# Gated cross-attention and mixture-of-experts block on one core: how the first context chunk, the positions and the later context chunks are loaded and split

## The chip, the core and the metric

The kernel runs on one core of a Trainium2 chip. The metric is device time in microseconds (us). TensorE (PE) multiplies matrices, VectorE (DVE), ScalarE (ACT) and GpSimd (POOL) do elementwise work, SyncE (SP) issues most DMAs. Each engine has its own queue of instructions and they meet at semaphores.

## The reference, cut to what matters

```python
x   = x + tanh(g_xattn) * xattn(layernorm(x), ctx, ctx, positions, mask, Wq, Wk, Wv, Wo)
x   = x + tanh(g_ffn)   * ffn(layernorm(x), gate_w, gate_b, w1, b1, w2, b2)

# xattn: x and ctx are [8, 128, 512]; 32 query heads, 8 key/value heads of 128; all fp32
q = (query @ Wq)                    # Wq [512, 4096]
k = (ctx @ Wk); v = (ctx @ Wv)      # Wk, Wv [512, 1024]
cos, sin = cos_t[position_ids], sin_t[position_ids]   # tables of 512 positions
q, k = q * cos + rotate_half(q) * sin, k * cos + rotate_half(k) * sin
attn = softmax(where(mask == 0, -1e9, q @ k.T / sqrt(128)))
xattn = (attn @ v) @ Wo             # Wo [4096, 512]
# ffn: three experts (tanh, gelu, silu) of 512x512 matrices, two of them chosen for each sample
```

The positions matter below only through the gather of their rows of the cos/sin table (rope).

## The kernel before

Every fp32 matrix is split into a high half (a copy rounded to fp32r by ACT or DVE) and a low half (the value minus the high half, by DVE or POOL). A product is then three matmuls: high by high, low by high, high by low. Names with `_hi` and `_lo` belong to these, and so do the semaphores: `c_hi` and `c_lo` count context chunks, `w_hi` and `w_lo` weight chunks.

The context comes as eight chunks (`ctx_in`), each 128 channels by 4 samples by 128 tokens: chunks one to four are the four parts of the contraction for samples 0 to 3, five to eight those for samples 4 to 7. SP loads them into four buffers `rows` (256 KB each), ACT and DVE split them into `cT` (a part of `big`). Weights come in chunks of 128 by 512 into four buffers `wraw` and are split into `wa` and `wb` (parts of `big` too). ACT issues the load of Wv's first chunk itself, and SP all other loads.

PE starts with `BLANKS` dummy matmuls on a zeroed tile (L562), then `first_values` forms the values of samples 0 to 3 in four banks (`y0`, `y1` and the two halves of `s`), chunk by chunk, so that each chunk is used when it comes:

```python
for c in range(EC - 1):
    pe.wait_ge(c_hi, c + 1)
    pe.wait_ge(w_hi, c + 1)
    if c == 0:
        pe.wait_ge(w0_half, 1)
    for b in range(BH):
        part(c, b, 0, 0)
    pe.wait_ge(c_lo, c + 1)
```

Then come 23 tiles of keys and values in an order written out by hand (`TILE_ORDER`): one value tile, then the first key tile, which has `rope_transpose(0)` and `(1)` ahead of it and `(2)` and `(3)` behind it. These are transposes of the gathered table rows, which POOL brings with eight indirect DMAs (L1161), four into `rot` and four into `prob`; the gathers wait for `pos_ok`, which DVE raises after four small operations on the positions (L1320 to L1327). All the rest of the program, 64 units of attention and then the experts, follows on PE in a fixed order.

Of the kernel before, what the change touches and what calls it, by code (L numbers as in the profile page):

```python
# [37 lines left out]
P = 128  # L38
B = 8
E = 512  # L40
EC = E // P
# [24 lines left out]
FILL = LAG_S  # L66
BLANKS = 9
LN_AT = (7, 11, 13, 14)
# [21 lines left out]
def build(nc, x, ctx_in, pos, mask, g_xattn, g_ffn, Wq, Wk, Wv, Wo, gate_w, gate_b, w1, b1, w2, b2,  # L90
          rope_rows, k_scratch, v_scratch, out):
    with ExitStack() as stack:
# [6 lines left out]
        def sem(name):  # L99
            return stack.enter_context(nc.semaphore(name))  # L100
# [57 lines left out]

        c_in = [sem(f"c_in{k}") for k in range(NROW)]
        c_hi, c_lo = sem("c_hi"), sem("c_lo")  # L160
        x_in = [sem(f"x_in{b}") for b in range(B)]
        small_in = sem("small_in")
        pos_in = sem("pos_in")
        mask_in = sem("mask_in")
        w_in = [sem(f"w_in{k}") for k in range(NW)]
        w_hi, w_lo, w0_half = sem("w_hi"), sem("w_lo"), sem("w0_half")
        pool_const, ident_ok, blank_ok = sem("pool_const"), sem("ident_ok"), sem("blank_ok")
# [100 lines left out]
        def piece(s, k):  # L268

            half, c = k // EC, k % EC  # L270
            return cT[s][half][:, :, c, :]

        def staged(k):
            return rows[:, k % NROW, :].rearrange("p (b t) -> p b t", b=BH)

# [125 lines left out]
        def _(sp):  # L401
# [5 lines left out]
            def c_load(k):  # L407
                if k >= NROW:
                    sp.wait_ge(c_lo, k - NROW + 1)
                sp.dma_start(rows[:, k % NROW, :], ctx_in[k // EC, k % EC]).then_inc(c_in[k % NROW], 16)  # L410

            for k in range(EC):
                c_load(k)
                if k >= 1:
                    w_load(k, w_chunks[k]).then_inc(w_in[k % NW], 16)
                else:
                    sp.dma_start(posi[:, :], pos).then_inc(pos_in, 16)
            for n in range(EC, W_DVE):
# [4 lines left out]
            for m in range(-AHEAD, TILES_A):  # L423
# [4 lines left out]
                if m < 0:  # L428
                    continue
                if m < B:  # L430
                    sp.dma_start(xacc[:, m, :], x[m]).then_inc(x_in[m], 16)
                if m == B:
# [73 lines left out]
        def _(pe):  # L506
# [21 lines left out]
            def first_values():  # L528
# [5 lines left out]
                for c in range(EC - 1):  # L534
                    pe.wait_ge(c_hi, c + 1)
                    pe.wait_ge(w_hi, c + 1)
                    if c == 0:
                        pe.wait_ge(w0_half, 1)
                    for b in range(BH):
                        part(c, b, 0, 0)  # L540
                    pe.wait_ge(c_lo, c + 1)
                    for b in range(BH):
                        part(c, b, 1, 0)
                    pe.wait_ge(w_lo, c + 1)
                    for b in range(BH):
                        part(c, b, 0, 1)
# [290 lines left out]
        def _(act):  # L837
# [27 lines left out]
            def c_hi_(k):  # L865
                act.wait_ge(c_in[k % NROW], 16 * (k // NROW + 1))
                act.activation(piece(0, k), staged(k), ACT.Copy).then_inc(c_hi, 1)
# [22 lines left out]

            act.dma_start(wraw[:, 0, :], w_chunks[0]).then_inc(w_in[0], 16)
            c_hi_(0)
            act.wait_ge(w_in[0], 16)
            act.activation(w_target(0)[0][0][:, 0, 0:256], wraw[:, 0, 0:256], ACT.Copy).then_inc(w0_half, 1)
            act.wait_ge(w_hi, 1)
# [381 lines left out]
        def _(dve):  # L1277
# [31 lines left out]
            def w_lo_(n):  # L1309
# [4 lines left out]
            dve.wait_ge(w_in[0], 16)  # L1314
            dve.tensor_copy(w_target(0)[0][0][:, 0, 256:512], wraw[:, 0, 256:512]).then_inc(w_hi, 1)
            c_lo_(0)
            dve.wait_ge(w0_half, 1)
            w_lo_(0)
            dve.wait_ge(pos_in, 16)
# [8 lines left out]
                              ).then_inc(pos_ok, 1)  # L1328

            for k in range(1, EC):  # L1330
                c_lo_(k)
                w_lo_(k)
# [480 lines left out]
```

## Time and profile before

| | |
|---|---|
| median of 3 runs | 701.52 us (701.26 to 702.04) |
| the profiled execution, its own time | 702.05 us |
| its span, first to last instruction | 700.3 us |
| PE busy | 691.8 us, 99% |
| DVE, ACT, POOL busy | 559.9, 361.4, 402.7 us |
| mean granted clock of PE | 0.997 |

The profile is of one execution, and its own time stands beside the runs. A row of the timeline gives an instruction's start, its duration, its engine and line, and in brackets how long the engine stood idle before it and who released it. A matmul of 512 columns is shown with a duration longer than its share of the pipeline, so that the spacing of starts says how fast PE goes.

### The profile page before, as it was taken

What the parts mean: (1) busy time and instruction counts of PE and PEld (TensorE: products, weight loads), DVE (VectorE), ACT (ScalarE), POOL (GpSimd) and SP (SyncE); (2) the same over time, 40 slices, a digit from 0 to 9 for tenths busy, and PEclk for the clock granted to TensorE, in tenths of its full rate; (3) what the DMA queues carried; (4) which work ended last, traced back from release to release, by engine and by line L of the source; (5) the groups of instructions that cost most, each with busy time, mean ns of one, the idle gap of its engine ahead of it and who ended that gap; (6) DMA issues with size and microseconds to landing.
All of it is one profiled execution on the core that took longest, in us unless ns stands there. A gap on an engine that the chain in (4) does not pass through costs nothing.

```text
span 700.3 us, 11567 instructions
## 1 busy us (share of the span) xinstructions
PE 691.8 (99%) x3479; PEld 580.2 (83%) x3479; DVE 559.9 (80%) x951; ACT 361.4 (52%) x961; POOL 402.7 (57%) x345
## 2 busy tenths in 40 slices
PE   9999999999999999999999999999999999999998
PEld 7888887888888888888888888888888887688886
DVE  5788786887887887887887887887887997687785
ACT  5525624545545545545555555555555687653521
POOL 5788855666666666666666566666566655330000
PEclk9999999999999999999999999999999999999999
DMA  8997564321231221221221221222222422120001
GB/s 264 345 307 287 196 205 141 107 89 61 63 91 61 62 90 60 64 86 60 66 84 62 67 83 60 68 82 60 72 80 61 136 90 76 60 77 31 1 31 60
DMA packets 65071, 70.84 MB, mean 101 GB/s; under 512 B 7680, under 2 KB 41472, under 8 KB 65024
## 3 DMA queue, kind: packets, MB, share of 16 engines
q1 hardware_dynamic: 64496, 68.98, 30.6%
q0 software_dynamic: 384, 1.05, 0.5%
q8 instruction: 19, 0.31, 0.2%
q10 hardware_dynamic: 144, 0.26, 0.1%
q14 instruction: 28, 0.23, 0.1%
HBM read 51.40 MB, written 18.87 MB: 100 GB/s over the span
## 4 chain that ended last, share of the span: by engine, by line
PE 89%; DVE 4%; ACT 2%; POOL 1%; issue 1%; SPq 1%; DMA 1%; DVEq 0%; ACTq 0%; POOLq 0%
PE q L298 29%; PE y L288 28%; PE q L288 6%; PE o L665 6%; PE s L647 5%; PE pt L509 4%; PE s L649 2%; PE o L288 2%; PE pt L288 2%; PE s L288 1%; PE s L509 1%; PE y L531 1%; PE s L531 1%; ACT prob L980 1%; DVE split L1279 1%
## 5 line engine op out<-in xcount | busy, mean ns | idle before, releaser
L288 PE MATMUL y<-big,split 128*128 128x512 f32 (+1 forms) x864 | 209.4, 391 | 0.7 <-DVE split L1279 0.5
L288 PEld LDWEIGHTS y<-big,split 128*128 128x128 f32 x864 | 161.0, 188 | 34.6 <-DVE split L1279 1.6
L298 PE MATMUL q<-xT_hi,big 128*128 128x512 f32 x512 | 175.1, 403 | 0.0
L1217 POOL TENSOR_TENSOR roped<-rot 128x512 f32<-128x512 f32 x58 | 75.1, 1294 | 101.7 <-DVE rot L1305 101.7
L966 ACT ACTIVATE big<-roped 128x512 fp32r<-128x512 f32 x63 | 40.0, 635 | 141.6 <-POOL roped L1217 136.4
L298 PEld LDWEIGHTS q<-xT_hi,big 128*128 128x128 f32 x512 | 96.1, 188 | 19.2
L980 ACT ACTIVATE prob<-scores,nmax 128x128 f32<-128x128 f32 x256 | 99.8, 391 | 20.4 <-DVE nmax L1437 20.3
L1231 POOL TENSOR_TENSOR prob<-prob,prec 128x512 f32<-128x512 f32 x64 | 66.7, 1042 | 60.5 <-DVE prec L1442 60.5
L298 PE MATMUL q<-xT_lo,big 128*128 128x512 f32 x256 | 99.5, 389 | 0.0
L1220 POOL TENSOR_TENSOR big<-roped,big 128x512 fp32r<-128x512 f32 x63 | 81.7, 1297 | 13.2 <-ACT big L966 13.2
L1209 POOL TENSOR_TENSOR big<-wraw,big 128x512 fp32r<-128x512 f32 x64 | 83.1, 1298 | 0.0
L1442 DVE RECIPROCAL prec<-psums 128x4 f32<-128x4 f32 x64 | 11.4, 178 | 66.1 <-ACT prob L980 65.8
L647 PE MATMUL s<-kv,big 128*128 128x256 f32 x256 | 62.6, 322 | 0.2 <-POOL big L1220 0.2
L949 ACT ACTIVATE split<-o 128x512 fp32r<-128x512 f32 x57 | 34.0, 597 | 54.3 <-PE o L665 54.3
L1301 DVE TENSOR_TENSOR rot<-q,rope 128x512 f32<-128x512 f32 x72 | 49.1, 682 | 10.6 <-PE q L298 8.8
L649 PE MATMUL s<-kv,big 128*128 128x128 f32 x256 | 57.0, 223 | 0.0
L1167 POOL TENSOR_TENSOR big<-wraw,big 128x512 fp32r<-128x512 f32 x32 | 41.1, 1296 | 27.0 <-ACT big L841 27.0
L298 PEld LDWEIGHTS q<-xT_lo,big 128*128 128x128 f32 x256 | 48.4, 189 | 8.7
L665 PE MATMUL o<-split,kv 128*128 128x512 f32 x192 | 54.4, 391 | 0.6 <-DVE split L1279 0.6
L1446 DVE SCALAR_TENSOR_TENSOR xacc<-y,gates,xacc 128x512 f32<-128x512 f32 x64 | 47.9, 748 | 5.2 <-PE y L288 1.2
L647 PEld LDWEIGHTS s<-kv,big 128*128 128x128 f32 x256 | 48.2, 188 | 3.3 <-POOL big L1220 0.8
L649 PEld LDWEIGHTS s<-kv,big 128*128 128x128 f32 x256 | 48.8, 191 | 2.4
(200 smaller groups left out, 1279.5 us busy)
## 6 DMA issues: line engine op xcount, KB each, us to landing
wraw<-in_L_xattn_Wq SPq DMA_DIRECT2D x32, 256.0 KB, 2.9
wraw<-in_L_xattn_Wo SPq DMA_DIRECT2D x32, 256.0 KB, 2.8
kv<-k_scratch SPq DMA_DIRECT2D x64, 128.0 KB, 2.5
kv<-v_scratch SPq DMA_DIRECT2D x64, 128.0 KB, 2.7
v_scratch<-split SPq DMA_DIRECT2D x12, 512.0 KB, 3.9
wraw<-in_L_ffn_w SPq DMA_DIRECT2D x24, 256.0 KB, 2.8
k_scratch<-split SPq DMA_DIRECT2D x10, 512.0 KB, 3.4
k_scratch<-kv SPq DMA_DIRECT2D x6, 512.0 KB, 3.5
```

Source lines behind the costliest of these rows:

```text
L288: mm = pe.matmul(bank_[:, :], stationary(s, c), moving(m, c), start=(c == 0 and n == 0), stop=(c == EC - 1 and n == 2))
L298: mm = pe.matmul(bank_[:, :].rearrange("p (b t) -> p b t", b=BH), weights[s][:, c, h * P:(h + 1) * P], source[m][:, half * BH:(half + 1) * ...
L647: pe.matmul(sbanks[:, 2 * h * P:(2 * h + 2) * P], q[0], kv[:, bs % NKV, 0:2, :].rearrange("p m k -> p (m k)"), start=True, stop=False)
L649: mm = pe.matmul(sbanks[:, 2 * h * P:(2 * h + 1) * P], q[1], kv[:, bs % NKV, 0, :], start=False, stop=True)
L665: mm = pe.matmul(obank[:, :], kv[:, bs % NKV, 2 + s, :], split[:, 1, m, :], start=(n == 0), stop=(n == 2))
L980: a = act.activation(prob[:, 0, h * P:(h + 1) * P], scores[:, h * P:(h + 1) * P], ACT.Exp, bias=nmax[:, turn, h:h + 1], accum_out=psums[:, ...
L1209: pool.tensor_tensor(buf[1][:, b % EC, :], wraw[:, b % NW, :], buf[0][:, b % EC, :].bitcast(F32), ALU.subtract).then_inc(w_lo, 1)
L1217: pool.tensor_tensor(roped[:, :], rot[:, 0, :], rot[:, 1, :], ALU.add).then_inc(q_roped, 1)
L1220: pool.tensor_tensor(q_split(1, bq // BH, bq % HG), roped[:, :], q_split(0, bq // BH, bq % HG).bitcast(F32), ALU.subtract).then_inc(q_lo, 1)
L1231: pool.tensor_tensor(heads(prob[:, 1, :]), heads(prob[:, 0, :]), prec[:, turn, :].unsqueeze(2).to_broadcast([P, HG, P]), ALU.mult).then_in ...
L1301: dve.tensor_tensor(to[:, 0, :], bank_[:, :], table(0, 0, D), ALU.mult)
L1446: dve.scalar_tensor_tensor(out=xacc[:, b3, :], in0=ybank[b3 % 2][:, :], scalar=gates[:, 0:1], in1=xacc[:, b3, :], op0=ALU.mult, op1=ALU.ad ...
```

## The change

It does six things.

- The first context chunk comes in two DMAs of 256 columns (samples 0 and 1, samples 2 and 3), with semaphores of their own (`c0_in`, `c_in[0]`), and ACT copies the halves one by one (`c0_half`, then `c_hi`).
- DVE makes the whole high half of Wv's first chunk (before, ACT and DVE made 256 columns each) and its low half at once behind it.
- PE takes the first chunk's products in another order: samples 0 and 1 high by high, then high by low, then the same of samples 2 and 3, then all four low by high.
- DVE handles the positions behind chunk two (index 1) instead of ahead of it; SP issues their load behind both halves of chunk one.
- Context chunks five to eight go into `xacc` (four of the buffers that later take x), so SP does not wait for a free buffer in `rows`; the loads of x into these four wait for `c_lo` instead.
- There are 7 dummy matmuls instead of 9.

```diff
-BLANKS = 9
+BLANKS = 7
...
         def staged(k):
-            return rows[:, k % NROW, :].rearrange("p (b t) -> p b t", b=BH)
+            return (rows[:, k, :] if k < NROW else xacc[:, k - NROW, :]).rearrange("p (b t) -> p b t", b=BH)
...
             def c_load(k):
-                if k >= NROW:
-                    sp.wait_ge(c_lo, k - NROW + 1)
-                sp.dma_start(rows[:, k % NROW, :], ctx_in[k // EC, k % EC]).then_inc(c_in[k % NROW], 16)
-
-            for k in range(EC):
+                sp.dma_start(staged(k), ctx_in[k // EC, k % EC].rearrange("p (b t) -> p b t", b=BH)
+                             ).then_inc(c_in[k], 16)
+
+            sp.dma_start(rows[:, 0, 0:2 * P], ctx_in[0, 0][:, 0:2 * P]).then_inc(c0_in, 16)
+            sp.dma_start(rows[:, 0, 2 * P:4 * P], ctx_in[0, 0][:, 2 * P:4 * P]).then_inc(c_in[0], 16)
+            sp.dma_start(posi[:, :], pos).then_inc(pos_in, 16)
+            for k in range(1, EC):
                 c_load(k)
-                if k >= 1:
-                    w_load(k, w_chunks[k]).then_inc(w_in[k % NW], 16)
-                else:
-                    sp.dma_start(posi[:, :], pos).then_inc(pos_in, 16)
+                w_load(k, w_chunks[k]).then_inc(w_in[k % NW], 16)
...
                 if m < B:
+                    if m < PIECES - NROW:
+                        sp.wait_ge(c_lo, NROW + m + 1)
                     sp.dma_start(xacc[:, m, :], x[m]).then_inc(x_in[m], 16)
...
                 for c in range(EC - 1):
-                    pe.wait_ge(c_hi, c + 1)
                     pe.wait_ge(w_hi, c + 1)
                     if c == 0:
-                        pe.wait_ge(w0_half, 1)
+
+                        pe.wait_ge(c0_half, 1)
+                        part(c, 0, 0, 0)
+                        part(c, 1, 0, 0)
+                        pe.wait_ge(w_lo, c + 1)
+                        part(c, 0, 0, 1)
+                        part(c, 1, 0, 1)
+                        pe.wait_ge(c_hi, c + 1)
+                        part(c, 2, 0, 0)
+                        part(c, 3, 0, 0)
+                        part(c, 2, 0, 1)
+                        part(c, 3, 0, 1)
+                        pe.wait_ge(c_lo, c + 1)
+                        for b in range(BH):
+                            part(c, b, 1, 0)
+                        continue
+                    pe.wait_ge(c_hi, c + 1)
...
             act.dma_start(wraw[:, 0, :], w_chunks[0]).then_inc(w_in[0], 16)
-            c_hi_(0)
-            act.wait_ge(w_in[0], 16)
-            act.activation(w_target(0)[0][0][:, 0, 0:256], wraw[:, 0, 0:256], ACT.Copy).then_inc(w0_half, 1)
+            act.wait_ge(c0_in, 16)
+            act.activation(piece(0, 0)[:, 0:2, :], staged(0)[:, 0:2, :], ACT.Copy).then_inc(c0_half, 1)
+            act.wait_ge(c_in[0], 16)
+            act.activation(piece(0, 0)[:, 2:4, :], staged(0)[:, 2:4, :], ACT.Copy).then_inc(c_hi, 1)
             act.wait_ge(w_hi, 1)
...
             dve.wait_ge(w_in[0], 16)
-            dve.tensor_copy(w_target(0)[0][0][:, 0, 256:512], wraw[:, 0, 256:512]).then_inc(w_hi, 1)
+            dve.tensor_copy(w_target(0)[0][0][:, 0, :], wraw[:, 0, :]).then_inc(w_hi, 1)
+            w_lo_(0)
+            dve.wait_ge(c0_half, 1)
             c_lo_(0)
-            dve.wait_ge(w0_half, 1)
-            w_lo_(0)
+            c_lo_(1)
+            w_lo_(1)
             dve.wait_ge(pos_in, 16)
...
-            for k in range(1, EC):
+            for k in range(2, EC):
                 c_lo_(k)
                 w_lo_(k)
```

On DVE, at the start of the program; `wraw` is a weight chunk as loaded, `rows` a context chunk, `posf` and `posi` the positions. Before:

```order
L1315 CAST big<-wraw 128x256 [waits w_in0]
L1279 TENSOR_TENSOR big<-rows,big 128x4x128 [waits c_hi]
L1279 TENSOR_TENSOR big<-wraw,big 128x512 [waits w_hi,w0_half]
L1320 CAST posf<-posi 128x8 [waits pos_in]
L1322 TENSOR_SCALAR posf<-posf 128x8 [waits pos_step]
L1325 TENSOR_TENSOR posf<-posf 128x8 [waits pos_step]
L1327 TENSOR_SCALAR posi<-posf 128x8 [waits pos_step]
L1279 TENSOR_TENSOR big<-rows,big 128x4x128 [waits c_hi]
L1279 TENSOR_TENSOR big<-wraw,big 128x512 [waits w_hi]
```

The same place after the change:

```order
L1333 CAST big<-wraw 128x512 [waits w_in0]
L1297 TENSOR_TENSOR big<-wraw,big 128x512 [waits w_hi]
L1297 TENSOR_TENSOR big<-rows,big 128x4x128 [waits c_hi,c0_half]
L1297 TENSOR_TENSOR big<-rows,big 128x4x128 [waits c_hi]
L1297 TENSOR_TENSOR big<-wraw,big 128x512 [waits w_hi]
L1340 CAST posf<-posi 128x8 [waits pos_in]
L1342 TENSOR_SCALAR posf<-posf 128x8 [waits pos_step]
L1345 TENSOR_TENSOR posf<-posf 128x8 [waits pos_step]
L1347 TENSOR_SCALAR posi<-posf 128x8 [waits pos_step]
```

Wv's low half has moved ahead of the context's, and the four operations on the positions stand behind two more subtractions.

On PE, from the dummies to the end of the first chunk. Before:

```order
L562 MATMUL o<-xT_hi 128x512 [waits blank_ok]
L562 MATMUL o<-xT_hi 128x512 x8
L531 MATMUL y0<-big 128x512 [waits w0_half,w_hi,c_hi]
L531 MATMUL y1<-big 128x512
L531 MATMUL s<-big 128x512 x2
L531 MATMUL y0<-big 128x512 [waits c_lo]
```

And after:

```order
L579 MATMUL o<-xT_hi 128x512 [waits blank_ok]
L579 MATMUL o<-xT_hi 128x512 x6
L533 MATMUL y0<-big 128x512 [waits c0_half,w_hi]
L533 MATMUL y1<-big 128x512
L533 MATMUL y0<-big 128x512 [waits w_lo]
L533 MATMUL y1<-big 128x512
L533 MATMUL s<-big 128x512 [waits c_hi]
L533 MATMUL s<-big 128x512 x3
L533 MATMUL y0<-big 128x512 [waits c_lo]
```

The banks `y0` and `y1` (samples 0 and 1) now get two products each before `s` (samples 2 and 3) gets its first. Behind the chunk nothing moves on PE.

On SP, the first issues of the program. Before:

```order
L410 DMA rows<-ctx_t 128x512
L417 DMA posi<-in_pos_BxS2 128x8
L410 DMA rows<-ctx_t 128x512
L405 DMA wraw<-in_L0_xattn_Wv 128x512
...
L410 DMA rows<-ctx_t 128x512 [waits c_lo] x4
L405 DMA wraw<-in_L0_xattn_Wk 128x512 [waits w_lo] x7
L431 DMA xacc<-in_x 128x512
```

And after:

```order
L412 DMA rows<-ctx_t 128x256
L413 DMA rows<-ctx_t 128x256
L414 DMA posi<-in_pos_BxS2 128x8
L409 DMA rows<-ctx_t 128x512
L406 DMA wraw<-in_L0_xattn_Wv 128x512
...
L409 DMA xacc<-ctx_t 128x512 x4
L406 DMA wraw<-in_L0_xattn_Wk 128x512 [waits w_lo] x7
L433 DMA xacc<-in_x 128x512 [waits c_lo]
```

One issue has come in ahead of chunk two, and the four context loads have lost their wait.

## Rows read from the trace of the kernel before

**Rows 1.** Totals of the page: busy time, share of the span, instructions.

```profile
PE 691.8 (99%) x3479; PEld 580.2 (83%) x3479; DVE 559.9 (80%) x951; ACT 361.4 (52%) x961; POOL 402.7 (57%) x345
```

**Rows 2.** Waits of PE in 0 to 50 us: total, times, longest.

```profile
PE o L562 <- POOL xT_hi L1141: 1.4, 1, 1.4
```

**Rows 3.** The chain that ended last, 0 to 24.7 us: start, duration, what.

```profile
1.39 4.21 PE o L562 x9
5.60 1.15 PE y L531 x2
...
7.36 0.47 PE y L531 x2
```

**Rows 4.** Timelines of 0 to 45 us, several engines (q: issuing a DMA).

```profile
4.66 0.29 DVE L1315 CAST big<-wraw 128x256 fp32r<-128x256 f32 x1 [4.66 <-DMA wraw<-in_L_xattn_Wv]
5.02 0.40 ACT L894 ACTIVATE big<-wraw 128x256 fp32r<-128x256 f32 x1
5.53 0.50 PEld L531 LDWEIGHTS y<-big 128*128 128x128 f32 x2 [0.66 <-ACT big L867]
5.86 4.97 SPq L410 DMA_DIRECT2D rows<-ctx_t  x4
6.36 0.16 DVE L1320 CAST posf<-posi 128x8 f32<-128x8 int32 x1
7.08 0.63 ACT L841 ACTIVATE big<-wraw 128x512 fp32r<-128x512 f32 x1
7.76 0.68 DVE L1279 TENSOR_TENSOR big<-wraw,big 128x512 fp32r<-128x512 f32 x1
10.88 9.64 SPq L405 DMA_DIRECT2D wraw<-in_L_xattn_Wk  x7
```

**Rows 5.** Context chunks one and two: loads issued at 0.82 and 1.73, us to landing.

```profile
rows<-ctx_t SPq DMA_DIRECT2D x1, 256.0 KB, 3.6
rows<-ctx_t SPq DMA_DIRECT2D x1, 256.0 KB, 4.7
```

**Rows 6.** Timeline of POOL, 7 to 22 us.

```profile
7.43 1.48 POOL L1161 DMA_INDIRECT rot<-rope_rows,posi  x1 [4.11 <-DVE posi L1327]
...
12.23 0.95 POOL L1161 DMA_INDIRECT rot<-rope_rows,posi  x1 [0.30 <-issue]
...
17.47 1.11 POOL L1161 DMA_INDIRECT prob<-rope_rows,posi  x1 [0.31 <-issue]
21.78 2.55 POOL L1167 TENSOR_TENSOR big<-wraw,big 128x512 fp32r<-128x512 f32 x2 [3.20 <-ACT big L841]
```

**Rows 7.** Timeline, PE's weight loads of the two pairs of rope transposes.

```profile
19.71 0.59 PEld L509 LDWEIGHTS pt<-ident,rot 128*128 128x128 f32 x4
...
23.36 0.58 PEld L509 LDWEIGHTS pt<-ident,prob 128*128 128x128 f32 x4
```

**Rows 8.** Loads issued at 12.23, 17.47, 19.0 and 20.5: us to landing.

```profile
rot<-rope_rows,posi POOLq DMA_INDIRECT x1, 7.1
prob<-rope_rows,posi POOLq DMA_INDIRECT x1, 3.8
wraw<-in_L_xattn_Wk SPq DMA_DIRECT2D x1, 256.0 KB, 3.0
xacc<-in_x SPq DMA_DIRECT2D x1, 256.0 KB, 4.8
```

**Rows 9.** Stretches: PE, PEld, DVE, ACT, POOL busy, granted clock, DMA share, GB/s.

```profile
18.00:19.00 1.00, 1.00 (x6) 0.83 (x5) 1.00 (x3) 1.00 (x4) 0.58 (x1) 1.00 0.78 281
21.00:22.00 1.00, 1.00 (x6) 0.79 (x6) 0.36 (x1) 0.64 (x2) 0.22 (x1) 1.00 0.87 227
```

**Rows 10.** The same columns, three stretches around 600 us.

```profile
595.00:598.00 3.00, 2.18 (x14) 1.06 (x13) 2.19 (x5) 2.77 (x6) 0.00 (x1) 1.00 0.24 90
604.25:607.66 3.41, 3.41 (x9) 2.64 (x8) 2.10 (x16) 2.15 (x3) 0.00 (x0) 0.50 0.28 79
607.66:611.00 3.34, 3.34 (x16) 2.74 (x15) 1.94 (x3) 2.62 (x5) 1.39 (x2) 1.00 0.00 0
```

More of the change, by code:

```diff
@@ L155, in bank_user @@
             return n - 4 if n < 3 * BH + 2 else n - 2
-        c_in = [sem(f"c_in{k}") for k in range(NROW)]
+        c_in = [sem(f"c_in{k}") for k in range(PIECES)]
         c_hi, c_lo = sem("c_hi"), sem("c_lo")
+        c0_in, c0_half = sem("c0_in"), sem("c0_half")
         x_in = [sem(f"x_in{b}") for b in range(B)]
@@ L165, in build @@
         w_in = [sem(f"w_in{k}") for k in range(NW)]
-        w_hi, w_lo, w0_half = sem("w_hi"), sem("w_lo"), sem("w0_half")
+        w_hi, w_lo = sem("w_hi"), sem("w_lo")
         pool_const, ident_ok, blank_ok = sem("pool_const"), sem("ident_ok"), sem("blank_ok")
@@ L865, in c_hi_ @@
             def c_hi_(k):
-                act.wait_ge(c_in[k % NROW], 16 * (k // NROW + 1))
+                act.wait_ge(c_in[k], 16)
                 act.activation(piece(0, k), staged(k), ACT.Copy).then_inc(c_hi, 1)
```

## Prediction

> **What bounds the kernel now.** I read the totals first: TensorE (PE) is busy 691.8 of 700.3 us [rows 1], so the change can only pay where PE stands still, where its clock is slow, or where it creates a wait. The list of PE's waits over the first 50 us [rows 2] has one entry, 1.4 us for the memset that the dummies read: after it PE waits for nothing. The chain of the first 25 us [rows 3] shows the same from the other side: it is PE alone after 1.39. Nine dummy matmuls take 4.21 us, 0.47 each; the first two real ones take 1.15, and a pair from 7.36 on 0.47, which is 0.23 each. So PE runs at the slow level (1.2 GHz) up to about 6.9 us and at the fast one (2.4 GHz) after it, though the clock column, which has no record so early, prints 1.00 there. A gain at the start is therefore a gain of the whole, but a small one; and whatever makes PE wait later in these 25 us is paid in full.
>
> **The start, worked out.** PE's first real weight load is at 5.53 [rows 4]; its 0.66 us of waiting lies under the last dummies. What ends last for it is ScalarE's (ACT) half of Wv's first chunk: 5.02 + 0.40 = 5.42, so from release to load it is 0.11. After the change PE needs two things. One is the first half of the context chunk: the whole chunk is there at 0.82 + 3.6 = 4.4 [rows 5], half of it not later, and ACT's copy of 256 columns took 0.40 [rows 4], so at 4.9 at worst. The other is VectorE's (DVE) cast of all 512 columns of Wv, which can start at 4.66 as now. Casts of 8 and of 256 columns took 0.16 and 0.29 [rows 4]; the line through them gives 0.42 at 512. Bounds: 0.29, and the 0.68 of a subtraction of 512. I take 0.42, the same operation: the cast ends at 5.08 and PE loads at 5.2, 0.33 earlier (0.07 to 0.46).
> That is at the slow level, where a matmul takes 0.43 and 0.33 us is three quarters of one; at the end it is worth 0.75 x 0.23: **-0.2 us** (0 to -0.4). The seven dummies are issued within 7 x 0.47 = 3.3 us of 1.39, by 4.7, so they don't hold PE up.
> Do the next passes find their data? The low half of Wv is ready at 5.1 + 0.7 = 5.8, and PE asks for it with its third matmul, two slow ones (1.0 to 1.15) after 5.2. The second half of the chunk is issued an SP slot after the first, at 1.27, and with the 3.6 of the whole chunk lands at 4.9; its copy ends at 5.3, wanted by the fifth matmul at about 7.0. The chunk's low half is ready at 6.5, wanted by the ninth, after 7.8. All free; with the cover gone they would cost one for one.
> Then chunk two. SP now issues one DMA more ahead of it, a slot of 0.46 us (1.27 to 1.73), so it lands between 1.73 + 4.7 = 6.4 [rows 5] and 6.9. ACT's two copies of 0.63 [rows 4] end at 8.2 at the latest, and PE, after 12 matmuls, wants them at 8.85. Slack 0.6, cost 0.
>
> **Context chunks five to eight.** SP no longer waits for DVE ahead of each: the four are issued from about 5.1 to 6.9 instead of over 4.97 us from 5.86, and the first Wk chunk right behind instead of at 10.88 [rows 4]. PE waits for none of these today, so this is worth 0 by itself. The new waits of SP ahead of the first four x loads count c_lo, and are met before SP comes to them: the Wk loads ahead wait for low halves that DVE writes after all eight steps of c_lo. 0 as well. What it does change is who shares the DMA engines when.
>
> **The positions.** This is the step that costs. Today the four small operations on the positions stand behind the first chunk, from 6.36 [rows 4], and GpSimd (POOL) starts the first of its eight gathers of rope rows 1.07 later, at 7.43 [rows 6]. Now they stand behind chunk two's two subtractions. Those are released by ACT's copies: if chunk two lands as today, they end at 7.76 + 0.68 = 8.44 [rows 4]; if one SP slot later, at 8.9. That is 2.1 to 2.5 us after 6.36, and every gather moves by it.
> Who is waiting? PE's transposes of the gathered rows. The first pair loads at 19.71, the second at 23.36 [rows 7]. The eighth gather is issued at 17.47 and lands 3.8 later, at 21.3 [rows 6, 8]: 2.1 us before PE wants it. Moved by 2.1 to 2.5 it lands at 23.4 to 23.8, while PE, 0.2 ahead, wants it at 23.15: a new wait of 0.2 to 0.7 us. How long a gather takes depends on what else is moving: an x load issued behind the Wk loads, at 10.88 + 9.64 = 20.5 [rows 4] and so in the middle of where gather eight will be, took 4.8 [rows 8]. The DMA engines are a little busier at 21 to 22 us (0.87) than at 18 to 19, where gather eight is under way now (0.78) [rows 9], so I take 3.8 to 4.3 and not 4.8: landing at about 23.8, **wait +0.7 us** (0 to 1.7, the end with 4.8 and the later chunk two). POOL stands still for 3.20 us behind its last gather until 21.78 [rows 6], more than the gathers move, so POOL's own work is not held.
> The spacing of the gathers may not stay either. The first, issued while DVE works without a pause, took 1.48; the fourth took 0.95 and the last 1.11 [rows 6], and DVE will now work on under more of them. I keep today's 10.04 us from first to last, because the fourth, too, has DVE subtractions beside it; two more as slow as the first would add twice 0.5. The Trainium skill (GPSIMD Engine Reference, "1. Specifications") says that POOL shares its SBUF interfaces with VectorE and contends with DVE instructions that have two SBUF inputs; by that rule the wait would be near 1.7 and not 0.7. The 1.48 agrees with it, the fourth's 0.95 does not.
> Sum: -0.2 + 0.7 = **+0.5 us**. Nothing behind gives that back, since PE is what the later chains start from. The profiled execution took 702.05 us by its own time (span 700.3); the median of the runs shown is 701.52, 0.5 below it. Added to the median: 702.0.
>
> **Rivals.**
> *The gathers are in time.* With context chunks five to eight long gone by the time of gather eight, it could take little more than the 3.0 of a Wk chunk of twice its bytes issued at 19.0 [rows 8], and be there by 22.9 to 23.1. Then only the start is left: 701.3. Against it: the x load's 4.8.
> *The fourth gather is late* (the other side). Today it is issued at 12.23 and takes 7.1 us [rows 6, 8], landing 0.4 before the first pair of transposes at 19.71. Issued at 14.5 and as slow as that, it lands at 21.6, 2.1 us after PE asks: with the -0.2, +1.9 and 703.4. It decides once the gather takes over 5.0 us. Against it: those 7.1 stand behind four Wk chunks that SP issued in a row from 10.88, which now go out earlier or one by one.
> *The fast clock comes later.* Today PE is busy without a break from 1.39 up to the rise. Now it is empty from about 4.7 to 5.2. If the rise slips for that, more is done at the slow level. Its price has a row: in 3.41 us at granted 0.50 PE did 9 matmuls, in the next 3.34 us at 1.00 it did 16 [rows 10]; as much again at the slow level costs 7 x 0.23 = 1.6 us. PE then comes to the transposes so late that the gathers cost nothing: -0.2 + 1.6 = +1.4, 702.9. Against it: with PE busy only 2.18 of 3.00 us at 595 the clock stayed at 1.00 [rows 10], though that is a fall not made and no rise. The Trainium skill (TensorE: Matmul & The Clock Gate, "Part 1: The HAM clock gate") says that the default is the throttled state and that activity releases it; by that rule fewer dummies and a hole speak against the change.
> *A slow stretch goes away.* The clock is at 0.50 from 604.25 to 607.66 [rows 10]; shifted against PE's work this could vanish, or the first rise could come sooner: -1.5, 700.0. Nothing in the change aims at it.
> *The start isn't earlier*: the two halves and the Wv chunk share the DMA engines, and Wv lands later by what the extra packets cost, or chunk two misses 8.85. Then the change does not do what it says; the gathers' wait shrinks as much, 701.6 to 702.2.
>
> **How the numbers follow.** Gather eight makes PE wait (702.0; its own range 701.3 to 702.8): 0.52. Gathers in time (701.3): 0.22. Later rise (702.9): 0.10. Fourth gather (703.4): 0.07. Slow stretch gone (700.0): 0.04. Start not earlier: 0.05. A difference under 0.2%, 1.4 us, is about what cannot be told from no change; that is 700.1 to 702.9. Below lies only the vanished stretch, 0.04. Above lie the fourth gather and a good half of the later rise, 0.13. The rest is no change, 0.83. The range 701.0 to 703.0 leaves out the fourth gather, the vanished stretch and the upper part of the rise, together under 0.2.
>
> **What would show it.** DVE's cast of Wv at 0.4 us and PE's first real load near 5.2. The first gather at 9.5 to 10.0. A wait of PE ahead of the transposes that read prob, of 0.2 to 1.2 us, and none ahead of those that read rot. The spacing of 0.23 from about 6.9 on. Wrong would be: gather eight down by 23.1 (then the gain stays), a wait before the first pair of transposes, slow matmuls after 7.5, or a wait of PE at chunk two.

## The result, and the profile after

| | before | after |
|---|---|---|
| median of 5 runs each, taken together | 702.04 us (701.26 to 703.29) | 705.67 us (704.44 to 707.27) |
| after over before | | 1.006 [1.0046, 1.0074] |
| the profiled execution, its own time | 702.05 us | 707.27 us |
| its span | 700.3 us | 705.5 us |
| mean granted clock of PE in it | 0.997 | 0.995 |

The change makes the kernel 3.6 us slower, outside the predicted range (701.0 to 703.0) and on the side that had a chance of 0.13. The profiled execution is the slowest of the five, so its 5.2 us are 1.6 more than the medians show. (A ratio and its interval are taken over all the runs and need not equal the quotient of the medians.)

Totals of the page, columns as in [rows 1]:

```profile
PE 692.2 (98%) x3477; PEld 579.9 (82%) x3477; DVE 560.3 (79%) x951; ACT 361.2 (51%) x961; POOL 402.4 (57%) x345
```

PE has two dummies less and is busy 0.4 us longer, in a span that is 5.2 longer: most of the loss is time in which PE stands still. Waits of PE in 0 to 50 us, which answer to [rows 2]:

```profile
PE pt L511 <- DMA prob<-rope_rows,posi: 3.7, 1, 3.7
PE o L579 <- POOL xT_hi L1159: 1.4, 1, 1.4
PE y L533 <- ACT big L858: 0.2, 1, 0.2
```

The memset's 1.4 is the old entry. The 3.7 is new: the second pair of rope transposes waits for a gather. The chain of this stretch (start, duration, what) follows it back:

```profile
20.18 6.45 DMA prob<-rope_rows,posi
26.62 0.04 issue
26.67 1.12 PE pt L511 x4
27.78 0.85 PE o L511 x4
28.64 4.52 PE q L299 x12
```

Gather eight took 6.45 us from its issue to landing, where before it took 3.8 [rows 8]. And the work behind it is slow: twelve matmuls in 4.52 us are 0.38 each instead of 0.23. Timelines of the first 27 us (start, duration, engine and line, what, in brackets the idle time before it and its releaser), which answer to [rows 4, 6, 7]:

```profile
4.20 0.43 DVE L1333 CAST big<-wraw 128x512 fp32r<-128x512 f32 x1 [4.20 <-DMA wraw<-in_L_xattn_Wv]
4.68 0.44 PEld L533 LDWEIGHTS y<-big 128*128 128x128 f32 x2 [0.66 <-DVE big L1333]
7.49 0.63 ACT L858 ACTIVATE big<-wraw 128x512 fp32r<-128x512 f32 x1 [0.17 <-DMA wraw<-in_L_xattn_Wv]
8.77 0.17 DVE L1340 CAST posf<-posi 128x8 f32<-128x8 int32 x1
9.85 1.36 POOL L1179 DMA_INDIRECT rot<-rope_rows,posi  x1 [6.53 <-DVE posi L1347]
19.20 0.60 PE L511 MATMUL pt<-ident,rot 128*128 128x128 f32 x4
19.36 0.43 SPq L433 DMA_DIRECT2D xacc<-in_x  x1
20.18 0.94 POOL L1179 DMA_INDIRECT prob<-rope_rows,posi  x1 [0.30 <-ACT big L858]
20.55 0.43 SPq L433 DMA_DIRECT2D xacc<-in_x  x1
21.03 0.66 SPq L378 DMA_DIRECT2D v_scratch<-split  x1
26.67 1.12 PE L511 MATMUL pt<-ident,prob 128*128 128x128 f32 x4 [3.70 <-DMA prob<-rope_rows,posi]
```

The start does what was forecast: the cast takes 0.43, and PE's first real load is at 4.68 where it was at 5.53. The first gather moves by 2.4 us, from 7.43 to 9.85, the eighth by 2.7, from 17.47 to 20.18. What was not forecast stands around it: x is loaded from 19.36 on (before, from 20.55), and the store of the values follows at 21.03. Two loads and a store, issued at 19.36, 20.55 and 21.03 (the last figure is us to landing):

```profile
xacc<-in_x SPq DMA_DIRECT2D x1, 256.0 KB, 5.7
...
xacc<-in_x SPq DMA_DIRECT2D x1, 256.0 KB, 6.0
...
v_scratch<-split SPq DMA_DIRECT2D x1, 512.0 KB, 6.9
```

All of them are slow together with the gather: the x load that took 4.8 [rows 8] takes 5.7. Stretches, with the columns of [rows 9]:

```profile
16.00:18.00 2.00, 2.00 (x10) 1.66 (x9) 2.00 (x4) 2.00 (x5) 1.70 (x2) 1.00 0.41 118
...
25.49:32.31 6.82, 5.64 (x18) 4.77 (x19) 0.44 (x1) 2.86 (x5) 2.77 (x3) 0.50 1.05 403
32.31:36.00 3.69, 3.69 (x18) 3.04 (x17) 2.68 (x4) 0.00 (x0) 0.56 (x1) 1.00 1.05 407
604.00:608.00 4.00, 4.00 (x22) 2.06 (x19) 3.33 (x9) 2.48 (x6) 1.30 (x1) 1.00 0.00 0
```

At 16 to 18 us the DMA engines are busy only 0.41, where before they were at 1.05: the loads have been brought forward. From 20 to 24 they are at 0.86 and 0.91, about as before (0.85 and 0.95). So the share alone does not say why the gather is slow; what is new is that it is issued among these loads. From 25.49 to 32.31 the granted clock is 0.50 (1.2 GHz), before and behind it 1.00 (2.4 GHz). PE had been waiting since 22.97 when it fell. The stretch at 604 to 608, at 0.50 in the trace of before [rows 10], is at 1.00 here.

### The profile page after: what moved, and what is told of

It is laid out like the page before. It is cut to its first block, busy times and chain, and to the rows that moved or that the text cites. A ratio compares the mean times of both kernels' runs of the same rounds, so it can differ in the third digit from the quotient of the medians.

```text
span 705.5 us, 11564 instructions
## 1 busy us (share of the span) xinstructions
PE 692.2 (98%) x3477; PEld 579.9 (82%) x3477; DVE 560.3 (79%) x951; ACT 361.2 (51%) x961; POOL 402.4 (57%) x345
## 3 DMA queue, kind: packets, MB, share of 16 engines
q0 software_dynamic: 384, 1.05, 0.4%
## 4 chain that ended last, share of the span: by engine, by line
PE 84%; DVE 6%; DMA 3%; ACT 2%; issue 2%; SPq 2%; POOL 1%; DVEq 0%; ACTq 0%; POOLq 0%
PE q L299 28%; PE y L289 27%; PE q L289 6%; PE o L682 6%; PE s L664 5%; PE pt L511 4%; PE s L666 2%; PE o L289 2%; PE pt L289 2%; PE s L511 1%; DMA prob<-rope_rows,posi 1%; DMA wraw<-in_L_xattn_Wv 1%; PE s L289 1%; DVE split L1297 1%; ACT prob L998 1%
## 5 line engine op out<-in xcount | busy, mean ns | idle before, releaser
L998 ACT ACTIVATE prob<-scores,nmax 128x128 f32<-128x128 f32 x256 | 99.8, 391 | 20.6 <-DVE nmax L1456 20.5
```

The lines of the kernel that those rows point to most:

```text
L998: a = act.activation(prob[:, 0, h * P:(h + 1) * P], scores[:, h * P:(h + 1) * P], ACT.Exp, bias=nmax[:, turn, h:h + 1], accum_out=psums[:, ...
```

## The experiments

The chip's runs show, for every kernel, a spread of some 3 us; part of it is a slow-clock stretch of 3.41 us near 603 to 613 that some executions have and some don't, so each ratio is taken over 11 or 12 runs of a kernel (6 for the repeat of the change) and 29 or 35 runs of the kernel before on the same chip. The time given is the median. Line numbers are those of each variant's own file and differ by a line or two.

**1. The change with the positions ahead of chunk two again.** The rest of the change stays.

```diff
             c_lo_(0)
-            c_lo_(1)
-            w_lo_(1)
             dve.wait_ge(pos_in, 16)
...
+            c_lo_(1)
+            w_lo_(1)
             for k in range(2, EC):
```

> The changed kernel with one step undone: DVE's four operations on the positions stand ahead of chunk two's subtractions again. Theory A (the late positions make the last gather late, and PE's 3.7 us wait for it also lets the clock fall): gathers start near 7.4, no wait of PE at the second pair of rope transposes, clock at 1.00 from the first rise on; time 701.3 to 702.0, 0 to 0.7 under the kernel before. Theory B (chunks five to eight, issued early, shift the weight and x loads so that these compete with the gathers): the last gather still lands behind 23.4 and most of the loss stays, 704 or more. Theory C (7 dummies): slow matmuls longer at the start, about 703.

Measured: 701.12 us, ratio to before 0.9977 [0.9966, 0.9987]. Two lines of DVE's order turn 0.6% slower into 0.2% faster. Its waits of PE in 0 to 50 us, and its chain:

```profile
PE o L579 <- POOL xT_hi L1159: 1.4, 1, 1.4
PE y L533 <- ACT big L858: 0.6, 1, 0.6
```

```profile
23.73 0.44 PE pt L511 x4
24.17 0.43 PE o L511 x4
24.60 2.74 PE q L299 x12
27.34 0.68 PE y L289 x3
```

The gather is waited for no more. This execution has a clock of 1.00 throughout and a span of 699.0, so it is the one to take the change's 705.5 apart by. In the chains the second pair of rope transposes starts at 23.73 here and at 26.67 in the change, 2.9 us later: the 3.7 of the wait, less about 0.7 by which the change came to them sooner. From the transposes to the end of the twelve matmuls behind them PE takes 27.34 - 23.73 = 3.6 us, in the change 28.64 + 4.52 - 26.67 = 6.5. So 2.9 us is the slow clock behind the wait. That is 5.8 of the 6.5. Another 0.5 is a later wait that this kernel lacks, 0.52 us for DVE ahead of the key tile at 60.88; 0.2 is left over.

**2. Before, with the positions moved alone.**

```diff
             w_lo_(0)
+            c_lo_(1)
+            w_lo_(1)
             dve.wait_ge(pos_in, 16)
...
-            for k in range(1, EC):
+            for k in range(2, EC):
```

> The kernel before with one part of the change: the positions behind chunk two's subtractions. Theory A: gathers 2 us later, the last lands at 23.2 or later, PE waits 0.2 to 3 us for it, time 702.5 to 705.5. Theory B: the gather is still in time, 702.0 as before.

Measured: 703.64 us, 1.0011 [0.9999, 1.0022]. The same move, which costs 0.7% in the change (experiment 9 against 10), costs about 0.1% here, and the interval reaches to none. The first gather starts at 9.37 and the eighth at 18.84, but the first x load is issued at 21.59, and PE comes to the second pair of transposes only at 24.7 (released by ACT, whose copies stood behind a late Wk chunk, and not by the gather). So a late gather is not enough; something else in the change makes it dear.

**3. The change, with context chunks five to eight in `rows` and their waits as before.**

```diff
-            return (rows[:, k, :] if k < NROW else xacc[:, k - NROW, :]).rearrange("p (b t) -> p b t", b=BH)
+            return rows[:, k % NROW, :].rearrange("p (b t) -> p b t", b=BH)
...
             def c_load(k):
+                if k >= NROW:
+                    sp.wait_ge(c_lo, k - NROW + 1)
...
-                    if m < PIECES - NROW:
-                        sp.wait_ge(c_lo, NROW + m + 1)
                     sp.dma_start(xacc[:, m, :], x[m]).then_inc(x_in[m], 16)
```

> The changed kernel with context chunks five to eight in the four buffers of rows again, with their waits. Theory A: loss stays, 704.5 to 706.5, PE's wait of 2 to 4 us stays. Theory B: the wait goes and the time is 701.5 to 702.5.

Measured: 703.34 us, 0.9998 [0.9982, 1.0013]. The loss is gone here too, by another way. In its timelines of ACT and PE:

```profile
16.30 0.63 ACT L884 ACTIVATE big<-rows 128x512 fp32r<-128x512 f32 x1 [1.79 <-DMA rows<-ctx_t]
```

```profile
18.41 3.01 PE L289 MATMUL y<-big 128*128 128x512 f32 x12 [0.95 <-DVE split L1297]
```

Chunk eight comes late. DVE frees the bank of the first value tile behind chunk eight's subtraction, and so the tile waits 0.95 us; the x loads go out from 21.66 on instead of 19.36. PE is then later at the transposes and the gather has less beside it, and PE does not wait for it (it waits 0.5 us there for a copy of ACT). The wait that the own buffers remove is real, and the one that they create is dearer.

**4. Before, with context chunks five to eight in `xacc` alone.**

```diff
-            return rows[:, k % NROW, :].rearrange("p (b t) -> p b t", b=BH)
+            return (rows[:, k, :] if k < NROW else xacc[:, k - NROW, :]).rearrange("p (b t) -> p b t", b=BH)
...
-                if k >= NROW:
-                    sp.wait_ge(c_lo, k - NROW + 1)
...
+                    if m < PIECES - NROW:
+                        sp.wait_ge(c_lo, NROW + m + 1)
                     sp.dma_start(xacc[:, m, :], x[m]).then_inc(x_in[m], 16)
```

> The kernel before with one part of the change: context chunks five to eight in buffers of their own, without waits. Theory A: no wait of PE, time within 0.4 of the kernel before. Theory B: the gathers are slowed by it, PE waits at a rope transpose, 703.5 or more.

Measured: 701.09 us, 0.9974 [0.9963, 0.9985]. What the prediction took for nothing is the one part that pays, and it pays as much as experiment 1 (701.12 beside it), which has the new start as well. The trace of before has no wait of PE here [rows 2], but experiments 2 and 3 have one, of 0.7 and 1.0 us, in the same place. In the profiled execution of before that DVE step ended at 16.82 and PE wanted the bank at 17.4; in experiments 2 and 3 PE starts 0.15 us behind that step, so the wait was missed by some 0.4 us. The runs of before reach higher (701.18 to 705.64 in 35 runs, this kernel 699.76 to 702.35 in 12), as they would if others had the wait; that is argued, since no trace of before shows it, and a wait of 0.7 to 1.0 us would not be all of the 1.6 us between the medians. ACT reads the later chunks without a wait for a DMA:

```profile
13.00 1.16 ACT L868 ACTIVATE big<-xacc 128x512 fp32r<-128x512 f32 x2 [0.57 <-issue]
```

**5. Before, with both: experiment 2's and 4's edits**, the old start and nine dummies.

```diff
-                if k >= NROW:
-                    sp.wait_ge(c_lo, k - NROW + 1)
...
             w_lo_(0)
+            c_lo_(1)
+            w_lo_(1)
             dve.wait_ge(pos_in, 16)
```

> The kernel before with both parts at once, the positions behind chunk two and chunks five to eight in buffers of their own, but the old start (whole first chunk, 9 dummies). Alone the first gave +0.1% and the second -0.26%. Theory D (the two interact: early context lets PE reach the transposes early and puts x loads and stores beside the late gathers): 704.5 to 706.5, with a wait of PE of 2 to 4 us for the last gather. Theory F (the new start is part of the loss): the two simply add, 701.5 to 702.5.

Measured: 704.24 us, 1.0029 [1.0014, 1.0043]. Alone the two edits give +0.11% and -0.26%, together +0.29%: 0.44% or 3.1 us comes from their meeting. The new start is not needed for the loss, though the whole change, with 0.41 and 0.60%, loses somewhat more. In the profiled execution (span 699.9) the eighth gather starts at 18.45, the first x load at 19.57, and PE does not wait: the gather's last packet moves at 22.1, 3.6 us behind its issue, and PE is at the transposes at 23.04. The same x, Wk and store issues follow this gather, but the first x load comes 1.1 us behind it, where in the change it came 0.8 ahead. So this trace shows the near miss and not the loss itself, which other runs of the kernel (up to 707.22) must have. That is argued from their times and clocks: the three slowest, 706.21 to 707.22, have a mean clock of 0.995, as the change's profiled execution has.

**6. The change, with the x loads held until all gathers have landed.**

```diff
                         sp.wait_ge(c_lo, NROW + m + 1)
+                    if m == 0:
+                        sp.wait_ge(rope_in[1], 16 * BH)
                     sp.dma_start(xacc[:, m, :], x[m]).then_inc(x_in[m], 16)
```

> The changed kernel with SP held ahead of the first x load until the second four gathers have landed, so that no x load, no store and no further weight load is issued beside the last gather. Theory D: the last gather takes 3.0 to 4.2 us instead of 6.45 and PE's wait at the second pair falls to 0.5 to 1.5 us; the time comes to 702 to 704 unless the held weight loads make a wait of their own. Theory E (a gather issued at 20.2 just takes that long, whatever runs beside it): it still lands behind 26 and the time is 705 or more.

Measured: 703.24 us, 1.0010 [0.9997, 1.0024]. Timelines of POOL, SP and PE:

```profile
20.26 0.94 POOL L1181 DMA_INDIRECT prob<-rope_rows,posi  x1 [0.30 <-issue]
```

```profile
23.91 0.33 SPq L435 DMA_DIRECT2D xacc<-in_x  x1
```

```profile
23.89 0.66 PE L513 MATMUL pt<-ident,prob 128*128 128x128 f32 x4
```

Nothing is issued between the gather at 20.26 and the x load at 23.91, which the landing releases (the last DMA ahead of the gather is a Wk chunk at 19.85): the gather takes at most 3.65 us, as late as in the change and 2.8 us faster. PE has no wait of its own at the transposes. The hold is not free: PE waits 1.54 us for DVE ahead of a key tile at 56.48, where the change had 0.52 at 60.88.

**7. The change, with each x load two tiles later.**

```diff
-                if m < B:
-                    if m < PIECES - NROW:
-                        sp.wait_ge(c_lo, NROW + m + 1)
-                    sp.dma_start(xacc[:, m, :], x[m]).then_inc(x_in[m], 16)
+                if 2 <= m < B + 2:
+                    if m - 2 < PIECES - NROW:
+                        sp.wait_ge(c_lo, NROW + m - 1)
+                    sp.dma_start(xacc[:, m - 2, :], x[m - 2]).then_inc(x_in[m - 2], 16)
```

> The changed kernel with each x load two tiles later, the stores where they are. Theory D: two loads of 256 KB less beside the last gather, which lands 0.7 to 1.5 us sooner; PE's wait 2 to 3 us, 703 to 705. Theory E: no difference, 705.7.

Measured: 702.44 us, 1.0005 [0.9991, 1.0019]. The gather still shares the DMA engines with a Wk chunk (20.63) and with the store of the values (21.00); the first x load is issued at 22.39. Chain and wait:

```profile
19.71 4.41 DMA prob<-rope_rows,posi
24.17 0.66 PE pt L511 x4
```

```profile
PE pt L511 <- DMA prob<-rope_rows,posi: 0.7, 1, 0.7
```

With the two x loads of 19.36 and 20.55 gone from beside it the gather takes 4.41 instead of 6.45, the wait is 0.7 instead of 3.7, and the clock stays at 1.00 behind it. These are close to what the prediction had for the change itself (3.8 to 4.3, a wait of 0.7, 702.0).

**8. The change, with 16 dummy matmuls ahead of the second pair of transposes**, so that PE works where it would wait.

```diff
                     if n == 0:
+                        for _ in range(16):
+                            pe.matmul(qbank[1][:, :], cT[0][0][:, 0, 0, :], wb[0][0][:, 0, :], start=True, stop=True)
                         rope_transpose(2)
```

> The changed kernel with 16 dummy matmuls (a free bank, 16 x 0.23 = 3.6 us) between the first key tile and the second pair of rope transposes, where PE waits 3.7 us. If the fall of the clock behind the wait is part of the loss: PE's wait all but vanishes from the list, the clock stays at 1.00 up to 600 us, and the time is 703.0 to 704.5 (1.2 to 2.7 less than the changed kernel in those runs where it fell). If the clock does not matter: 705.7.

Measured: 704.91 us, 1.0035 [1.0022, 1.0049]. Chain, and the stretch that was slow in the change:

```profile
23.42 3.63 PE q L599 x16
27.05 0.44 PE pt L511 x4
27.49 0.44 PE o L511 x4
```

```profile
25.49:32.31 6.82, 6.82 (x35) 5.71 (x35) 2.37 (x5) 2.76 (x5) 2.61 (x3) 1.00 1.05 407
```

35 matmuls in the same 6.82 us at 1.00, where the change, idle for the first 1.2 of them, did 18 at 0.50, the DMA engines as full in both. PE reaches the transposes 0.4 us later than in the change (27.05 against 26.67) and the execution ends 3.4 us sooner (span 702.1 against 705.5, neither with a slow stretch at 604): 2.9 of clock and the later wait of 0.5 that it lacks, less the 0.4, and 0.4 left over. So a fall of the clock behind an idle PE is a cost apart from the wait, and keeping PE busy avoids it. None of the 12 runs has a mean clock of 0.995, which 5 of the change's 11 have. The median is above the 703.0 to 704.5 expected, and its ratio can't be told from the repeat's 1.0041. The dummies take their 3.6 us in every run, also where the gather is sooner: in this execution its last packet moved at 25.2, so that PE would have waited some 2 us and not 3.6.

**9. The change, repeated**, on one chip with the next three.

> The changed kernel itself once more, beside the next three on one chip, since its 5 runs came from another call and no execution of it but one has a trace. Theory D: 0.4 to 0.7% over the kernel before, PE's wait at the second pair of rope transposes between 1 and 4 us, and executions whose mean clock is 0.995 (the fall behind that wait) among the slowest. If the loss was luck of those runs: under 0.2%.

Measured: 706.1 us, 1.0041 [1.0026, 1.0057]. Chain, wait and clock of a second execution:

```profile
19.48 6.32 DMA prob<-rope_rows,posi
25.84 0.98 PE pt L511 x4
```

```profile
PE pt L511 <- DMA prob<-rope_rows,posi: 2.7, 1, 2.7
```

```profile
26.02:29.43 3.41, 3.41 (x13) 3.02 (x13) 0.21 (x1) 2.92 (x5) 2.21 (x2) 0.50 1.06 408
```

The long gather and the fall of the clock are there again, the wait one us shorter and the slow stretch half as long. Three of the six runs have a mean clock of 0.995 and are the slowest, 706.45 to 707.22.

**10. Experiment 1 again**, beside the repeat.

> The changed kernel with the positions ahead of chunk two's subtractions, again, on the same chip as the changed kernel. Theory D: 3.5 to 5 us under the changed kernel, 0.15 to 0.3% under the kernel before, no wait for a gather.

Measured: 700.93 us, 0.9972 [0.9961, 0.9984]. On one chip, the two lines of DVE's order are worth 706.1 - 700.93 = 5.2 us.

**11. Experiment 1 with nine dummies.**

```diff
-BLANKS = 7
+BLANKS = 9
```

> The same with 9 dummies instead of 7. Theory C (fewer dummies and the hole behind them delay the fast clock): 0.5 to 1.5 us faster than with 7. Otherwise: 9 dummies end at 5.6 and hold PE up by 0.7 us at the slow level, but chunk two, which PE waits for anyway, hides it; within 0.3 us of the kernel with 7.

Measured: 701.47 us, 0.9980 [0.9969, 0.9991]. The interval overlaps that of seven dummies, so the two can't be told apart. The timeline of PE's weight loads gives a reason why the earlier start is worth so little:

```profile
4.97 1.26 PEld L533 LDWEIGHTS y<-big 128*128 128x128 f32 x4
```

In experiment 1 that load is at 4.68, 0.3 earlier, and PE then waits 0.6 us for Wv's second chunk; here it waits 0.2.

**12. The change, with the second pair of rope transposes behind the second key tile** (on ACT the copies of them are moved to match).

```diff
-                    if n == 0:
+                    if n == 1:
                         rope_transpose(2)
                         rope_transpose(3)
...
-                if m == BH + 2:
-                    rope_copy(2)
-                    rope_copy(3)
...
                     w_hi_to(W_DVE + m - 2)
+                if m == BH + 2:
+                    rope_copy(2)
+                    rope_copy(3)
```

> The changed kernel, positions late as in the change, but PE does the second key tile ahead of the second pair of rope transposes, 2.7 us of work in which the last gather can land. Theory D: PE's wait falls from 3.7 to 0 to 1.2 us, but DVE can turn the second key tile only behind those transposes, so some of it comes back as a wait for DVE; 702 to 704, under the changed kernel by 2 us or more. If PE's wait there is not what costs: 705.7.

Measured: 701.33 us, 0.9983 [0.9971, 0.9995]. Chain:

```profile
20.69 5.47 PE q L299 x24
26.16 0.44 PE pt L511 x4
26.59 0.44 PE o L511 x4
```

The late gathers stay, the traffic beside the gather stays (the x load issued with it takes 5.3 us, and the gather's last packet moves at 24.5, behind the 23.4 at which PE would have come to the transposes), and PE does the next tile's twelve matmuls instead of waiting. The whole loss is gone: 4.8 us against the repeat on the same chip. So the loss is the order on PE against the landing, with what follows on the clock, and not something that late gathers do elsewhere.

The fastest version is that of experiments 1 and 10, 0.2 to 0.3% below before; experiments 4 (without the new start), 11 and 12 can't be told from it.

## Why the prediction was wrong

**The place was right.** The cast took 0.43 (0.42 forecast). The first gather moved by 2.4 us (2.1 to 2.5 forecast). PE waits ahead of the transposes that read `prob` and not ahead of those that read `rot`. The rival with the fourth gather did not come about: those transposes are at 19.20 without a wait. Nor did the later rise of the clock: in the change 16 matmuls lie between 5.01 and 9.00, and their pairs are 0.46 us apart from 6.90 on. The trace's first record of the full clock is at 5.01, in that of before at 6.92. Over all fourteen traces it lies between 4.85 and 7.33, and the earliest is one with nine dummies and the old start (experiment 4).

**The term that failed is the wait: +0.7 us (0 to 1.7), with the gather taken at 3.8 to 4.3.** It took 6.45 and 6.32 us, and the wait was 3.7 and 2.7. The prediction took the price of the DMA engines' company from the trace of before, where Wk chunks and one x load at the gather's end are beside it. In the change four more transfers start within 1.7 us around the gather: x at 19.36, a Wk chunk, x at 20.55 and the store of 512 KB at 21.03. Experiments 6 and 7 price this: 3.65 us at most with nothing issued until it lands, 4.41 with a Wk chunk and the store, 6.3 to 6.5 with all in the two traces of the change. In experiments 8 and 12, with the same issues beside the gather, its last packet moves 5.4 and 4.8 us behind its issue (a landing is seen some 0.3 later), so the price is not a fixed one. In experiment 5, where the first x load comes 1.1 us behind the gather, it is 3.6. The four long gathers are those with an x load issued together with them or ahead of them, which the share of the DMA engines (0.86 against 0.85 at 20 to 22) does not show. Of the 1.7 that was the upper end, the x load's 4.8 was itself too low by the same error.

**The step behind that is "worth 0 by itself" for context chunks five to eight.** The prediction asked only whether PE waits for these loads in the one trace of before, where the wait was missed by some 0.4 us. It said that the edit changes "who shares the DMA engines when", and gave that no number. In fact SP's x loads and the store, and PE itself, move forward by about a microsecond (x from 20.55 to 19.36), toward gathers that move back by 2.7. Experiments 2, 4 and 5 separate the two: +0.11% and -0.26% alone, +0.29% together. And by itself the edit is worth 0.26%: a wait behind chunk eight, absent in the profiled execution of before, was present in those of experiments 2 and 3. That it is the whole gain isn't shown.

**The clock behind the wait was in no term.** Among the rivals the prediction argued that the clock had held at 595 with PE busy for 2.18 of 3.00 us [rows 10], but weighed that only for the first rise. Behind a wait of 3.7 us the clock fell to 0.50 for 6.82 us and cost 2.9; behind one of 2.7 it fell for 3.41; behind the 0.7 of experiment 7 it did not fall. Five of the change's 11 runs have a mean clock of 0.995, and they are the five slowest, 706.45 to 707.27. The other six, 703.85 to 705.75, have 0.997 to 0.999, as many runs of before have, so their loss is for the most part not the clock's. So the forecast wait was cheap and the real one not, beyond its own length. That activity releases the full clock and the throttled state is the default, as the Trainium skill has it (TensorE: Matmul & The Clock Gate, "Part 1: The HAM clock gate"), agrees with these three rows; the two fewer dummies and the hole in front of the first load, against which the prediction held the same rule, did nothing that the runs can tell (experiments 1 and 11).

**"Start: -0.2" was right as a shift and worth nothing.** PE's first real load is 0.85 earlier, more than forecast, since Wv's chunk was there at 4.20 in place of 4.66. But the slack of 0.6 at chunk two was wrong: PE was reckoned to want it at 8.85, and with the earlier start and the fast clock from about 5 it wants it at 7.97, while Wv's second chunk, behind one SP issue more, is copied at 7.49 + 0.63 = 8.12. PE waits there 0.2 us in the change, 0.6 in experiment 1 and 1.0 in experiment 6. Experiment 1 has the new start and experiment 4 the old one, with all else alike, and they are level (701.12 and 701.09). In the change's profiled execution PE does come to the tile ahead of the transposes 0.7 us sooner than before (19.99 against 20.73), with the clock's rise 1.9 us sooner.

**The gathers' spacing** was kept at 10.04 us from the first to the last. It is 20.18 - 9.85 = 10.33, since three of the eight took 1.36 to 1.45 and the others about 1.0. The rule on POOL's contention with VectorE (the Trainium skill, GPSIMD Engine Reference, "1. Specifications"), by which the wait would have been 1.7, adds 0.3 here and not the 1.0 that was reckoned for it. The slow ones lie beside DVE subtractions, but so do the last three, at 0.94 and 0.95 us, so the trace neither shows nor excludes the rule; in the repeat the sum is even smaller (19.48 - 9.98 = 9.50).

**The sum, redone by rows of the two profiled executions:** transposes 2.9 us later (23.74 to 26.67 in the chains: the wait of 3.7, one of 0.2 at chunk two, and some 0.9 gained at the start), slow clock behind them 2.9, later wait 0.5, small growth of two waits far behind (0.5 and 0.7 us where before had 0.2 and 0.6) 0.4, and the slow stretch at 604 that this execution lacks, -1.6: together 5.1 of the 5.2. The last of these is chance, which an execution has or has not.

**What stays open.** The traces show that the gather slows with what is issued beside it, not which of the transfers does it or by what means: the two x loads were only taken away or put off together. Why the gather is 1.3 us apart from trace to trace with the same issues beside it is open too. Why an execution of the changed kernel has 2.7 or 3.7 us of wait (runs from 703.85 to 707.27) was not settled, nor why the stretch near 604 comes and goes.

## What to carry to other kernels

Two edits that are each harmless can meet: when one makes a transfer later and the other makes the consumer or its neighbours on the DMA engines earlier, price the transfer by what will be issued around it after the change, not by its duration in the trace of before. A wait with no entry in one profiled execution may be there in others, so look by how much it was missed; the spread of the runs can hint at it. And where PE would wait, look for independent work of its own queue to put ahead (here the next tile's matmuls, 4.8 us for two moved calls), since a wait may cost the clock as well.

## What the runs showed of the hardware

- A gather of 128 rows, issued by POOL, takes 3.65 us at most from issue to landing when no other DMA is issued until it lands (a Wk chunk was issued 0.4 us ahead; experiment 6), 4.41 with a Wk chunk and a 512 KB store issued 0.9 and 1.3 us behind it (experiment 7), and 6.32 and 6.45 in the change, with two x loads of 256 KB as well, the first 0.0 and 0.8 us ahead of it. With that x load 1.1 us behind the gather its last packet moved after 3.6 us (experiment 5).
- In the change PE was idle from 22.97 to 26.67; the granted clock fell to 0.50 at 25.49 and stayed there until 32.31, although PE worked again from 26.67 on. Behind the repeat's wait of 2.7 it was at 0.50 for 3.41 us. With dummies in the wait it stayed at 1.00 (experiment 8), and behind a wait of 0.7 as well (experiment 7).
- Of the twelve executions profiled for the experiments, six have a slow-clock stretch of 3.41 us near 603 to 613 and six don't, and experiments 1 and 10, which are one kernel, differ in it; in the repeat it is the second row here (the first is a stretch at full clock, same columns as [rows 10]):

```profile
604.00:608.00 4.00, 3.92 (x24) 2.42 (x24) 2.46 (x9) 2.02 (x4) 2.09 (x2) 1.00 0.10 21
609.70:613.10 3.40, 3.40 (x10) 2.63 (x9) 2.43 (x15) 2.13 (x3) 0.00 (x0) 0.50 0.25 75
```
